# Wide cross attention reordered between two batches, softmax in halves; one shared chunk of a mixture moved, another mixture's vector work respread

## What is computed

```python
q = (h @ Wq).reshape(64, 16, 128)          # 16 heads of 128
k = repeat(ctx @ Wk, 2); v = repeat(ctx @ Wv, 2)   # ctx: 128 rows of 128, 8 kv heads
attn = nan_to_num(softmax(where(mask, q @ k.T / sqrt(128), -inf)))
x += (attn @ v) @ Wo
```

```python
shared = (silu(h @ sg) * (h @ su)) @ sd
p = softmax(h @ Wr); topw, sel = top_k(p, top); topw /= sum(topw)
x += shared + sum_j topw[j] * ((silu(h @ g[sel_j]) * (h @ u[sel_j])) @ d[sel_j])
```

## Time and profile before

| | us |
|---|---|
| profiled execution | 3307.98 |
| its span | 3305.9 |
| TensorE busy | 2821.2 (85%) |
| VectorE busy | 1872.1 (57%) |
| ScalarE busy | 1422.4 (43%) |
| GpSimd busy | 912.7 (28%) |
| one full-width pass (128 x 1024) of VectorE in the attention, L586 | 1.22 |
| one exp of that width, L556 | 1.06 |

### The profile page before, as it was taken

One profiled execution on the slowest core, in us unless ns is written; L12 is line 12 of the kernel. 1 busy time (PEld: TensorE's weight loads), 2 busy tenths in 40 slices (PEclk: granted clock), 3 DMA queues, 4 the chain that ended last, 5 costly groups with the idle time before them and its releaser, 6 DMA issues. The chain is left out here.

```text
span 3305.9 us, 47479 instructions
## 1 busy us (share of the span) xinstructions
PE 2821.2 (85%) x17712; PEld 1737.6 (53%) x17712; DVE 1872.1 (57%) x2415; ACT 1422.4 (43%) x2542; POOL 912.7 (28%) x742
## 2 busy tenths in 40 slices
PE   7999987889977988879997976557989798997997
PEld 5888872456654655633344632223654455553686
DVE  2333325412228954644458969667965799995342
ACT  3333325212236544532255645346557666652123
POOL 0111110013301532100003500000540699990362
PEclk9999998989998998989998998779999899999998
DMA  4000000501120000020000000000000111213124
GB/s 144 0 0 0 0 0 28 178 23 47 46 81 1 2 22 1 2 80 0 0 20 1 2 13 0 0 19 1 2 28 14 76 72 69 75 44 105 47 87 142
DMA packets 72132, 121.63 MB, mean 37 GB/s; under 512 B 10705, under 2 KB 53073, under 8 KB 71442
## 3 DMA queue, kind: packets, MB, share of 16 engines
q1 hardware_dynamic: 63026, 94.73, 8.6%
q0 software_dynamic: 8928, 24.39, 2.4%
HBM read 100.36 MB, written 18.74 MB: 36 GB/s over the span
## 5 line engine op out<-in xcount | busy, mean ns | idle before, releaser
L2999 POOL TENSOR_TENSOR h<-ssm_u,ss_bc 128x1024 f32<-128x1024 f32 x88 | 205.5, 2354 | 0.0
L2962 ACT ACTIVATE ssm_p_h<-ss_delta,ss_decay 128x256 f32<-128x256 f32 x352 | 146.5, 463 | 125.0 <-DVE ctxT L3036 84.6
L2911 PE MATMUL ssm_p_y<-ctxT,ident 128*128 128x512 f32 x412 | 187.6, 595 | 0.0
L604 POOL TENSOR_TENSOR xw_prob<-xw_prob,xw_rsum 128x1024 f32<-128x1024 f32 x32 | 60.7, 1896 | 419.0 <-DVE xw_rsum L591 419.0
L584 DVE TENSOR_REDUCE xw_nmax<-xw_p_s 128x8 f32<-128x1024 f32 x32 | 39.2, 1225 | 237.4 <-PE xw_p_s L515 237.4
L1320 POOL MEMSET ctxT<- 128x512 f32 x3 | 1.6, 526 | 591.3 <-POOLq L60 591.3
L3031 DVE TENSOR_TENSOR_SCAN ssm_p_h<-ssm_p_h,h 128x1024 f32<-128x1024 f32 x64 | 145.8, 2279 | 8.6 <-ACT ssm_p_h L2962 6.8
L2989 POOL TENSOR_TENSOR ctxT<-ctxT,ss_bc 128x1024 f32<-128x1024 f32 x50 | 117.2, 2351 | 16.5 <-DVE ctxT L3029 16.5
L2895 PE MATMUL ssm_p_h<-ssm_b_diagonal,ssm_uT 128*128 128x128 f32 x640 | 85.6, 290 | 40.5 <-DVE ctxT L3036 20.1
L2911 PEld LDWEIGHTS ssm_p_y<-ctxT,ident 128*128 128x128 f32 x412 | 76.5, 192 | 79.6 <-issue 78.5
L492 PE MATMUL xw_p_q<-h,xw_m_h 128*128 (+1 forms) x1024 | 117.0, 275 | 1.3 <-PEq L60 1.3
(11 more groups left out here) (740 smaller groups left out, 7154.6 us busy)
## 6 DMA issues: line engine op xcount, KB each, us to landing
ss_bc<-ss_bc_rows SPq DMA_DIRECT2D x24, 896.0 KB, 4.3
ss_bc<-ss_bc_rows SPq DMA_DIRECT2D x8, 768.0 KB, 4.1
L3f_rows<-L3f_rows_out SPq DMA_DIRECT2D x16, 384.0 KB, 3.9
L0f_wg<-in_L_ffn_gate SPq DMA_DIRECT2D x9, 512.0 KB, 10.1
L0f_wu<-in_L_ffn_up SPq DMA_DIRECT2D x9, 512.0 KB, 9.8
L0f_wd<-in_L_ffn_down SPq DMA_DIRECT2D x9, 512.0 KB, 9.9
L0f_rows<-L0f_rows_out SPq DMA_DIRECT2D x16, 256.0 KB, 4.0
x<-in_xT SPq DMA_DIRECT2D x1, 2048.0 KB, 7.5
```

The source lines that it names most:

```text
L604: g.tensor_tensor(prob[:, :, :], prob[:, :, :], bcast(rsum[:, 1, :], 2, S2), ALU.mult).then_inc(sem["normed"], 1)
L2911: mm = pe.matmul(p_y[:, 2 * half:2 * half + 2, :].rearrange("p e t -> p (e t)"), k.ident[:, :], weighed[n % RING_W][:, ts(half, CH)], star ...
L2962: i = act.activation(out[:, ts(e, CT)], delta[:, e, ts(c, CT)], ACT.Exp, scale=decay[:, E4 * s + e:E4 * s + e + 1])
L2999: g.tensor_tensor(tiles(drive[n % RING]), u[:, c % 2, :, :], bcast(bcs[:, row_b(s), :], 1, E4), ALU.mult).then_inc(sem["driven_g"], 1)
```

## The change

In the attention PE's order per batch becomes transposes of n, scores of n+1, mixing of n, projection; both bias matmuls come ahead of all scores; the softmax of a batch is done in two halves of four g each on DVE, ACT and GpSimd, each half with its own semaphore counts; `project_out` takes the heads in two halves; the masked context has two buffers and is made ahead of the maximum. Note that the bias is already a TensorE matmul in the kernel before. In the mixtures `LATE` is 3 for M = 4 and 4 for M = 2: with M = 4 the last shared chunk leaves the routing block and stands at the end of the queues of the expert blocks. The vector work of routing is spread by a table. The first RG loads of rows back are issued by SP inside the expert blocks' stage. The scratch banks p_x and p_h become one tile of two banks, which the late chunk uses.

```diff
             def project_out(i):
-                pe.wait_ge(sem["mixed_read"], 4 * i + 4)
+                for half in range(2):
+                    pe.wait_ge(sem["mixed_read"], 4 * i + 3 + half)
+                    for o in range(H2):
+                        for h in range(8 * half, 8 * half + 8):
...
+            def score(n, b, first=False):
+                if not first:
+                    pe.wait_ge(sem["shifted"], 2 * n)
+                for half in range(2):
+                    pe.matmul(p_s[:, 4 * half:4 * half + 4, :], ones_row[:, :], bcast(bias[:, ts(n, S2)], 1, 4),
+                              start=True, stop=False, skip_group_check=True)
+                for half in range(2):
+                    for g in range(4 * half, 4 * half + 4):
+                        mm = pe.matmul(p_s[:, g, :], qs[:, g, b, :], k.ctxT[:, ts(n, S2)], start=False, stop=True, skip_group_check=True)
+                    mm.then_inc(sem["scored"], 1)
+            def turn(n):
+                for half in range(2):
+                    pe.wait_ge(sem["normed"], 2 * n + half + 1)
+                    for g in range(4 * half, 4 * half + 4):
+                        mm = pe.transpose(p_t[:, half, ts(g % 4, P)], prob[:, g, :], k.ident[:, :])
+                    mm.then_inc(sem["turned"], 1)
+            def mix(n, b):
+                pe.wait_ge(sem["masked"], n + 1)
+                for half in range(2):
+                    pe.wait_ge(sem["turned_read"], 2 * n + half + 1)
+                    pe.matmul(p_u[:, half, :], ctxm[:, b, :], probT[:, ts(half, CH)], start=True, stop=True).then_inc(sem["mixed"], 1)
             def body(i, first=False, last=False):
...
+                if not first:
+                    project_out(i - 1)
+                turn(2 * i)
+                score(2 * i + 1, 1)
+                mix(2 * i, 0)
+                if not last:
+                    if not first:
+                        pe.wait_ge(sem["added"], i)
+                    project_q(i + 1)
+                turn(2 * i + 1)
+                if not last:
+                    pe.wait_ge(sem["q_copied"], 4 * i + 8)
+                    score(2 * i + 2, 0)
+                mix(2 * i + 1, 1)
             project_q(0)
+            pe.wait_ge(sem["q_copied"], 4)
+            score(0, 0, first=True)
...
+            def exponentials(n, half):
+                act.wait_ge(sem["shifted"], 2 * n + half + 1)
+                act.activation(prob[:, 4 * half:4 * half + 4, :], prob[:, 4 * half:4 * half + 4, :], ACT.Exp).then_inc(sem["exped"], 1)
...
+            def body(i, first=False, last=False):
+                n = 2 * i
+                if not first:
+                    mixed(n - 1, 1)
+                exponentials(n, 0)
+                exponentials(n, 1)
+                turned(n)
+                mixed(n, 0)
+                exponentials(n + 1, 0)
+                if not last:
+                    copy_q(i + 1, 0)
+                exponentials(n + 1, 1)
+                if not last:
+                    for q in range(1, 4):
+                        copy_q(i + 1, q)
+                turned(n + 1)
...
+            def soft(n, b, free):
+                if free:
+                    v.wait_ge(sem["mixed"], 2 * n - 2)
+                v.tensor_scalar(ctxm[:, b, :], ctxr[:, n, :], maskf[:, ts(n, 1)], None, ALU.mult).then_inc(sem["masked"], 1)
+                for half in range(2):
+                    part = slice(4 * half, 4 * half + 4)
+                    v.wait_ge(sem["scored"], 2 * n + half + 1)
+                    v.tensor_reduce(nmax[:, part], p_s[:, part, :], AX, ALU.max, negate=True).then_inc(sem["maxed"], 1)
+                    v.wait_ge(sem["maxed"], 2 * n + half + 1)
+                    v.tensor_tensor(prob[:, part, :], p_s[:, part, :], bcast(nmax[:, part], 2, S2), ALU.add).then_inc(sem["shifted"], 1)
+                for half in range(2):
+                    part = slice(4 * half, 4 * half + 4)
+                    v.wait_ge(sem["exped"], 2 * n + half + 1)
+                    v.tensor_reduce(rsum[:, 0, part], prob[:, part, :], AX, ALU.add).then_inc(sem["summed"], 1)
+                    v.wait_ge(sem["summed"], 2 * n + half + 1)
+                    v.reciprocal(rsum[:, 1, part], rsum[:, 0, part]).then_inc(sem["recip"], 1)
             def body(i, first=False):
...
+                soft(2 * i, 0, free=not first)
+                if not first:
+                    add_out(i - 1)
+                soft(2 * i + 1, 1, free=not first)
...
-                g.wait_ge(sem["recip"], n + 1)
-                g.tensor_tensor(prob[:, :, :], prob[:, :, :], bcast(rsum[:, 1, :], 2, S2), ALU.mult).then_inc(sem["normed"], 1)
+                for half in range(2):
+                    part = slice(4 * half, 4 * half + 4)
+                    g.wait_ge(sem["recip"], 2 * n + half + 1)
+                    g.tensor_tensor(prob[:, part, :], prob[:, part, :], bcast(rsum[:, 1, part], 2, S2), ALU.mult).then_inc(sem["normed"], 1)
+        LATE = NCH - 1 if M > 2 else NCH
...
-                for c in range(NCH):
+                for c in range(LATE):
                     if c == 0:
...
+                if M > 2:
+                    between = {0: [soften, lambda: pick(0)], 1: [lambda: pick(1)], 2: [gather_masks], 3: [weigh], 4: [place, own_blocks],
+                               6: [lambda: sort_out(0)], 8: [lambda: sort_out(1)]}
+                else:
+                    between = {0: [soften, lambda: pick(0)], 1: [lambda: pick(1)], 2: [lambda: pick(2), gather_masks], 3: [weigh], 5: [place],
+                               6: [own_blocks, lambda: sort_out(0)], 7: [lambda: sort_out(1)]}
+                for c in range(LATE):
                     for m in range(M):
+                        if M > 2 or c == 0:
+                            for part in between.get(M * c + m, ()):
+                                part()
                         shared_hidden(v, sem, p_u, M * c + m)
+                        if M == 2 and c > 0:
+                            for part in between.get(M * c + m, ()):
+                                part()
                     shared_add(v, sem, p_d, c)
+                if M == 2:
+                    sort_out(2)
                 make_lists()
         k.prefix = f"{layer}b_"
         s_y = [nc.alloc_semaphore(f"{k.prefix}block_stored{n}") for n in range(RY)]
+        s_g = [nc.alloc_semaphore(f"{k.prefix}rows_loaded{n}") for n in range(RG)]
+        back = rows[:, 0:RG * top, :].rearrange("p (t j) d -> p t j d", j=top)
+        by_tile = rows_out[0:top * T, :].rearrange("(j n p) d -> n p j d", j=top, p=P)
...
+            @block.sync
+            def _(sp):
+                for u in range(RY):
+                    sp.wait_ge(s_y[u], 16 * len(range(u, NB, RY)))
+                for t in range(RG):
+                    sp.dma_start(back[:, t, :, :], by_tile[t]).then_inc(s_g[t], 16)
...
+                for c in range(LATE, NCH):
+                    shared_pe(pe, late, p_g, p_u, p_d, c, first=LATE)
...
+                for c in range(LATE, NCH):
+                    for m in range(M):
+                        shared_hidden(v, late, p_u, M * (c - LATE) + m)
+                    shared_add(v, late, p_d, c, first=LATE)
...
+                act.wait_ge(sem["hidden"], NB)
+                for n in range(M * (NCH - LATE)):
+                    shared_act(act, late, p_g, n)
...
-            for u in range(RY):
-                sp.wait_ge(s_y[u], 16 * len(range(u, NB, RY)))
-            by_tile = rows_out[0:top * T, :].rearrange("(j n p) d -> n p j d", j=top, p=P)
-            for t in range(NT):
-                if t >= RG:
-                    sp.wait_ge(sem["combined"], t - RG + 1)
+            for t in range(RG, NT):
+                sp.wait_ge(sem["combined"], t - RG + 1)
                 sp.dma_start(back[:, t % RG, :, :], by_tile[t]).then_inc(s_g[t % RG], 16)
             if layer == "L3":
```

More of the change, by code:

```diff
@@ L548, in copy_q @@
                 act.copy(qs[:, 2 * q:2 * q + 2, :, :].rearrange("p g b t -> p (g b t)"), p_q[:, q % 2, :]).then_inc(sem["q_copied"], 1)
-            def body(i, last=False):
-                for b in range(2):
-                    n = 2 * i + b
-                    if b == 1 and not last:
-                        copy_q(i + 1, 0)
-                    act.wait_ge(sem["shifted"], n + 1)
-                    act.activation(prob[:, :, :], prob[:, :, :], ACT.Exp).then_inc(sem["exped"], 1)
-                    if b == 1 and not last:
-                        for q in range(1, 4):
-                            copy_q(i + 1, q)
-                    for half in range(2):
-                        act.wait_ge(sem["turned"], 2 * n + half + 1)
-                        act.copy(probT[:, ts(half, CH)], p_t[:, half, :]).then_inc(sem["turned_read"], 1)
-                    for half in range(2):
-                        act.wait_ge(sem["mixed"], 2 * n + half + 1)
```

(37 more changed lines are left out.)

75 lines of the change are left out of this document (18 added, 57 removed).

## The result

The changed kernel takes 3251.47 us (median of 4 runs, 3244.66 to 3253.09), the kernel before beside it 3308.93 us: ratio 0.9822, interval 0.9802 to 0.9841. 3247 was predicted, with a range of 3235 to 3270. A second measurement gave 3249.47 us and a ratio of 0.9830 (0.9817 to 0.9844). The profiled execution took 3252.89 us (span 3251.1), 55 less than the one of before. Medians and ratios, here and in the experiments, are of fast executions; one execution was slow (5432 us, softmax in one piece) and is left out of them.

The account below looks back on a forecast made before the run. TensorE was taken to bound wide attention, with holes in the mixtures' routing and block ends. Attention 34, L0 16, L3 routing 9.5 and L3 combine 2 sum to 61.5 us off 3307.98: 3247 us predicted, range 3235 to 3270.

Parts of the forecast that it names:

- Attention, steady: Wide attention, TensorE's period per batch: 12.4 us instead of 13.26, saving 26 us over thirty batches.
- rival 1: TensorE boundaries with a wait: each handover costs 0.1 us, 13 us less gain, 3260 us; chance 0.2.
- Rival 4: Wide attention: GpSimd's halves cost far more than half, the softmax chain sets the period, some 3321 us; chance 0.02.
- Head and tail: Wide attention's ends, where the softmax chain is bare: head gives 3 us, tail 5.
- L0: L0 mixture, last shared chunk moved: lists 25.8 us sooner, combine 11.5 later, net 17 or 15, taken as 16.
- The hole: End of L0's expert blocks: no transfer or engine busy for 6.1 us; the moved chunk should lie over it.
- rival 2: L0's hole stays uncovered because GpSimd's finish waits for all engines: 6 us less, cold combine, 3255 us; chance 0.1.
- the 2.8 us of a warm start: L0 combine: 14.3 us if TensorE starts warm, where it ran 17.10 with a cold start.
- L3 routing: L3 mixture, VectorE's placing and sorting spread over chunks 1 to 3: 9.5 us sooner (7 to 11).
- Rival 3: L3 routing: order only moves the wait to the last chunk, clock cold; gives 4, not 9.5, 3253 us; chance 0.07.
- L3's blocks: L3 expert blocks: no term of the sum gave them any change in time.
- L3 combine: L3 combine: returned rows loaded inside the block stage, so it waits only for scaled identities; 2 us sooner.

Follow-up runs that it names:

- experiment 6: Changed kernel with L0's last shared chunk back in the routing stage, spread sorting and early loads kept; ratio to the kernel before 0.9860.
- again: The changed kernel measured once more, unchanged, with a second profile: 3249.47 us, ratio to the kernel before 0.9830.
- mixtures only: Kernel before with the new sparse mixtures alone, wide attention as before: 3286.5 us, ratio to the kernel before 0.9948.
- softmax whole: Changed kernel with its softmax again in one piece of 128x1024, TensorE's new order kept; ratio to the kernel before 0.9874.
- biases apart: Changed kernel with each half's bias matmul again ahead of its own score products; ratio to the kernel before 0.9876.
- old order: Changed kernel with TensorE's attention order of before, softmax halves and biases together kept; ratio to the kernel before 0.9897.
- mask added: Changed kernel without bias matmuls, VectorE adding the mask to the scores: 3232.3 us, ratio to the kernel before 0.9789.
- Experiment 11: Changed kernel with L3's last shared chunk moved behind its expert blocks too, as in L0; ratio to the kernel before 0.9834.
- experiment 10: Changed kernel with filler identity matmuls in TensorE's idle stretches of both mixtures: 3256.3 us, ratio to the kernel before 0.9845.
- Experiment 7: Changed kernel with the loads of returned rows issued in the combine stage, behind the barrier, in both mixtures; ratio to the kernel before 0.9870.
- mask and warm: Changed kernel with the mask added by VectorE and resized filler matmuls in idle stretches: 3233.8 us, ratio to the kernel before 0.9762.
- Experiments 1 and 2: Kernel before with the new wide attention alone (3270.4 us, ratio 0.9902), and with the new mixtures alone (3286.5 us, ratio 0.9948).

## Why the prediction was right, step by step

**Attention, steady: the mechanism right, two terms 0.1 off against each other.** Period 12.31 and 12.33 for 12.4. Transposes 1.03 and 0.97 (0.91), the two biases to the first score 0.53 (0.75 with the switch), scores 1.89 (1.79), mixing 1.72 (1.7), projection 7.14 and 7.23 (7.23). The prediction let the second half of the scores end at the weight load at 261.25; the next matmul starts later. Timeline of the kernel before:

```profile
261.36 7.31 PE L492 MATMUL xw_p_q<-h,xw_m_h 128*128 x64
```

By this row that half takes 1.00 and not 0.89, and the 0.2 for a change to the bias, taken from 1.09 - 0.89, was too much: what stands ahead of the first bias now is 0.06 to 0.12 over the transposes' 0.91. In all the period fell by 0.94 and not 0.86, 28 us over thirty batches for 26. GpSimd's half, which no row before showed, took 1.04 us (taken 1.0, bounds 0.95 and 1.90). The handovers cost nothing, which sinks rival 1: TensorE shows no idle time at any boundary of the two batches. Rival 4 is sunk by the same 1.04 and the 2 us of slack.

**Head and tail: right.** 8 predicted, 9 left of attention's 37.3 behind the 28 (34 predicted in all); the wait for GpSimd in head and tail fell from 14.3 to 7.5 us, and the halves alone are worth 5.6.

**L0: the mechanism right, the sum 1 too high.** From its first gate the list matmuls came 25.8 us sooner, as worked out; the third gate waited 1.45 us (1.7 predicted). The combine started 11.75 us later (11.5). The hole is covered, so rival 2 is false, and experiment 6 puts a price on the move. Over the seven profiles with these mixtures and nothing else changed in L0 (after, again, mixtures only, softmax whole, biases apart, old order, mask added) the time from the gated scan's start to L1's is 452.7 on the mean, 450.2 to 455.0, against 467.6 and 468.3: 15.3 us. In the one execution that I compared first it was 12.9, and most of the difference is the lists, at a granted clock of 0.65. The combine itself did not get the 2.8 us of a warm start: 17.3 us for 18.3.

**L3 routing: right size, one cause wrong.** First gate to first gather 9.9 us sooner (9.5 predicted). I had VectorE's third sort as the bound; it ended at 3025.96, and TensorE's lists, unbroken to 3030.7, ended last. Counted from the router's first matmul it is 8.2 us, as transposes ahead of the first gate ran slower (24 records in 5.55 us at a granted clock of 0.51). Rival 3 does not hold: the wait did move to the last chunk (3.15 us), but the lists behind it ran warm. Experiment 11 shows what it would have been.

**L3's blocks: a cost that the prediction put at nothing.** They took 174.1 us from first gather to last store before and 173.9 with the new attention alone, but 176.2 to 176.7 in all nine profiles with the new mixtures that have no fillers and L3's routing as in the kernel after. 2.1 of it falls between the first transposes and the first store (13.1 us before, 15.1 now, 15.1 to 15.2 in all nine). Timeline of the second block's first matmul, kernel before and kernel after:

```profile
3098.03 1.12 PE L1000 MATMUL L3b_p_g<-L3f_wg,L3b_xT 128*128 x4 [0.60 <-DVE L3b_xT L1049]
```
```profile
3043.23 2.07 PE L1055 MATMUL L3b_p_g<-L3f_wg,L3b_xT 128*128 x4 [0.60 <-DVE L3b_xT L1109]
```

In the kernel before TensorE's granted clock was 1.00 again 6 us after the first transposes; in the kernel after it was still 0.50 for the three us from there. With fillers ahead of the transposes (experiment 10) the first store came after 11.0 us. So this is no scatter between executions; it comes with the new mixtures, and what in them holds the clock down longer is not shown.

**L3 combine: the size right, in part by luck.** 2.0 us sooner. Experiment 7 prices the loads under the hole at 3.4 there and 3.4 in L0, which I had not priced in L0 on its own. With the loads behind the barrier L3's end took 13.9, 14.9 and 15.3 us in three kernels, so the 2.0 is counted from the shortest of them.

**The sum.** 61.5 predicted, 54.8 in the first pair of profiles. Of the terms, attention gave 3 more and L0 3 less. The rest is in no term: 3.2 us between L1's start and L3's router, of which time mixing 2.8; 1.7 in L3's transposes ahead of the first gate; and 2.6 in L3's blocks. The 1.7 too is no scatter of one execution: router to first gate took 30.3 us in both profiles with the old mixtures and 32.0 in all with the new ones but mask and warm (30.3). So L3 in all, from its router to the end, gave 8.1 us where 11.5 were predicted, and the total is as close as it is partly because attention gave more. The trace of before had the shorter variant of time mixing, as two later kernels had it. My forecast took every stage outside its terms as fixed; between executions of one kernel some are not, by 3 us. Experiments 1 and 2 add to 49 us by ratio (1.5%), the whole change has 56 and 59; the intervals overlap, and the stages add to 64. So I take the parts as independent, which is not shown closer than that.

## What to carry to other kernels

Where an engine waits for a copy of its own result, put the next item's first step there: it was worth 0.5 us in 13.3, and it lengthened the cover of the softmax chain at the same time. Then look what else the bound engine does that another could: two short bf16 matmuls among fp32 ones cost 0.63 us a batch (12.32 less 11.69), and VectorE took them over under TensorE's work. Work moved over a wait is worth the wait that it covers, not its own length (20.5 won, 13.7 paid), and an idle stretch that it opens ahead of a long run of matmuls can cost more than it saves.

## What the hardware showed that I had not expected

- VectorE's 128x128 tensor_scalar from SBUF to SBUF does not share time with a GpSimd product: 0.28 us alone, 0.77 beside a 128x512 product, 1.75 beside one of 128x1024, ending within 0.1 us of it both times. Reductions of 128x512 beside the same product took 0.66 to 0.69 as ever. The Trainium skill, "GPSIMD Engine Reference", section "1. Specifications", says that the two engines contend for shared SBUF interfaces when VectorE's instruction has two SBUF inputs or a 2-port mode. The prediction drew from it that only this mask product could collide, and so it came; which of the two conditions it meets no run shows. By these rows it ends only when GpSimd's instruction does.
- After 9.37 us without work TensorE ran L3's 96 list records at a granted 0.50 (1.2 GHz) to their end, 20.7 us. With 3.15 us of idle time and the last chunk's projections in between, the same 96 ran at 0.99 in 10.97 us.
- A trace of one execution is good to about 3 us for some stages: the lists of L0 took 7.8 us (granted clock 0.91) or 10.8 (0.65), and time mixing 162.6 to 165.7, in kernels that do not differ there.
- How long TensorE stays at half clock after the same first matmuls is not fixed: in L3's blocks the clock was back at 1.00 by 6 us from the first transposes in both profiles with the old mixtures, and was 0.50 until 9 us in all ten with the new ones and no fillers.
- Fillers of the identity behind the same 1.38 us of idle time ran once at full clock (40 records in 4.70 us) and once at a granted 0.54 (28 in 5.79).
